# Dynamic weight builds of an attention + adapted FFN layer: every build group accumulated on DVE, DMA queue chosen by weight matrix instead of by parity

## The reference

```python
xn = layernorm(x)
out = x + attn(xn) + ffn(xn)

# attn: q, k, v = xn@wq, xn@wk, xn@wv; RMS norm over all 1024 of q and of k; 8 heads of 128;
#       each token sees itself and the 16 before it, ALiBi bias; softmax; (probs @ v) @ wo

# ffn, with weights of its own for every batch row:
h = relu(xn @ gate_w1.T + gate_b1)
g = (h @ gate_w2.T + gate_b2).mean(axis=1)          # (batch, 8)
mW1 = W1 + einsum('be,efh->bfh', g, TW1)            # 4096 x 1024, TW1 is (8, 4096, 1024)
mb1 = b1 + g @ Tb1
mW2 = W2 + einsum('be,ehf->bhf', g, TW2)            # 1024 x 4096, TW2 is (8, 1024, 4096)
mb2 = b2 + g @ Tb2
u = gelu(xn @ mW1.T + mb1)
ffn = u @ mW2.T + mb2
```

## Time and profile before

| | |
|---|---|
| time, median of 2 runs | 3646.16 us (3642.28 to 3650.03) |
| the profiled execution's own time | 3622.46 us |
| span of its slowest core, core 0 | 3620.6 us (all cores 3590.5 to 3620.6) |
| mean granted PE clock of the cores | 0.677 to 0.690 |
| busy on core 0: PE, DVE, ACT, POOL | 1204.2, 644.9, 658.7, 551.6 us |
| DMA | 475.37 MB, mean 131 GB/s |

### The profile page before, as it was taken

How to read it: one execution, slowest core, us unless ns; L and a number is a source line. 1 busy time by engine, 2 the same in 40 slices (tenths; PEclk the granted TensorE clock), 3 DMA queues, 4 the chain that set the end, 5 groups by cost and what they waited for, 6 DMA issues and landing times.

```text
span 3620.6 us, 18150 instructions; the slowest of 8 cores (3590.5 to 3620.6 us)
## 1 busy us (share of the span) xinstructions
PE 1204.2 (33%) x4955; PEld 491.3 (14%) x5044; DVE 644.9 (18%) x687; ACT 658.7 (18%) x1011; POOL 551.6 (15%) x267
## 2 busy tenths in 40 slices
PE   0333333523252326212622206000000065657565
PEld 0111111211020112100211002000000022222221
DVE  1010110222122212232132310222222200000000
ACT  1121211211222212122311122222222201011010
POOL 0000000011102210123011130344345300000000
PEclk9766666865675568555865558555555597979898
DMA  9222212043415340554034564887887746454544
GB/s 187 63 68 74 66 52 19 6 128 128 128 48 188 131 135 6 154 186 149 6 122 135 190 176 104 242 266 243 258 266 245 230 95 119 92 127 92 127 94 110
DMA packets 466039, 475.37 MB, mean 131 GB/s; under 512 B 362579, under 2 KB 362963, under 8 KB 465812
## 3 DMA queue, kind: packets, MB, share of 16 engines
q1 hardware_dynamic: 345060, 248.90, 24.9%
q10 hardware_dynamic: 116400, 214.81, 19.9%
q0 software_dynamic: 4480, 10.50, 1.9%
HBM read 357.91 MB, written 42.01 MB: 110 GB/s over the span
## 4 chain that ended last, share of the span: by engine, by line
DMA 27%; PE 26%; POOL 11%; DVE 10%; ACT 8%; SPq 7%; issue 6%; ACTq 5%; DVEq 0%; POOLq 0%
DMA O_s<-TW 15%; POOL accv_s L90 11%; SPq L95 7%; DMA O_s<-m2d 6%; PE pA L74 6%; ACTq L95 5%; PE pC L74 5%; PE pB L74 5%; PE pD L74 4%; PE pE L74 4%; PE pU L74 4%; DVE rz_s L90 3%; DVE accv_s L90 2%; DMA O_s<-xad 2%; DMA xnd<-xnb_s 2%
## 5 line engine op out<-in xcount | busy, mean ns | idle before, releaser
L90 POOL TENSOR_TENSOR accv_s<-bldt_s,accv_s 128x1024 f32<-128x1024 bf16 x224 | 477.9, 2133 | 2320.2 <-ACT bldt_s L85 2293.1
L85 ACT ACTIVATE bldt_s<-O_s,gbc_s 128x1024 bf16<-128x1024 f32 x256 | 293.0, 1147 | 1029.8 <-DMA O_s<-TW 573.5
L90 DVE SCALAR_TENSOR_TENSOR accv_s<-O_s,gbc_s,accv_s 128x1024 f32<-128x1024 f32 x224 | 287.7, 1284 | 754.8 <-DMA O_s<-TW 748.4
L74 PE MATMUL pA<-O_s 128*128 128x512 bf16 x624 | 194.4, 431 | 379.0 <-DMA O_s<-m1d 189.0
L74 PE MATMUL pA<-m2rowb_s,e0bf_s 128*128 128x512 bf16 x4 | 1.7, 428 | 636.8 <-DMA O_s<-m2d 633.2
L74 PE MATMUL pA<-O_s,selbf_s 128*32 128x512 bf16 x15 | 8.6, 571 | 554.0 <-ACT bldt_s L85 554.0
L74 PE MATMUL pB<-O_s 128*128 128x512 bf16 x631 | 179.6, 399 | 5.8 <-DMA O_s<-m2d 5.1
L90 DVE RECIPROCAL rz_s<-pE 1x512 f32<-1x512 f32 x32 | 104.9, 3314 | 375.5 <-PE pE L74 375.5
L74 PE MATMUL pC<-O_s,xt_s 128*128 128x512 bf16 x256 | 82.5, 480 | 242.3 <-DMA xt_s<-xnd 237.9
L85 ACT ACTIVATE O_s<-pA,mb_s 128x512 bf16<-128x512 f32 x64 | 44.0, 687 | 567.4 <-PE pA L74 564.2
L74 PEld LDWEIGHTS pA<-O_s 128*128 128x128 bf16 x640 | 65.9, 106 | 516.2 <-issue 473.2
(11 more groups left out here) (138 smaller groups left out, 1610.9 us busy)
## 6 DMA issues: line engine op xcount, KB each, us to landing
O_s<-TW ACTq DMA_DIRECT2D x256, 512.0 KB, 7.0
O_s<-TW SPq DMA_DIRECT2D x256, 512.0 KB, 5.6
O_s<-x SPq DMA_DIRECT2D x16, 1024.0 KB, 5.8
accv_s<-W SPq DMA_DIRECT2D x32, 512.0 KB, 5.5
accv_s<-W ACTq DMA_DIRECT2D x32, 512.0 KB, 5.0
xnd<-xnb_s ACTq DMA_DIRECT2D x32, 256.0 KB, 3.1
O_s<-x ACTq DMA_DIRECT2D x16, 512.0 KB, 3.6
xad<-O_s ACTq DMA_DIRECT2D x16, 512.0 KB, 2.8
```

Of the source, the lines that this page charges most:

```text
L74: i = self.eng.matmul(out, lhsT, rhs, start=start, stop=stop, skip_group_check=skip)
L85: i = self.eng.activation(out, in_, func, **kw) if self.on("scalar") else None
L90: i = getattr(self.eng, name)(*args, **kw) if self.on(who) else None
```

## The change

All groups now do their eight steps on DVE. The queue for a group's loads and store is SPq for the groups of `mW1` and ACTq for those of `mW2`. The `bldt` buffers go. Two accumulators, two output buffers and the ring of four slots stay. Apart from that, `gw1t` and `gb1r` get a semaphore of their own, `d_ldg2`, for which the gate's first matmul waits, and the wait for the rest of POOL's loads moves to `emit_g`.

```diff
@@ -30,7 +30,7 @@
 HS = HALO + SC
 
 SEM_NAMES = [
-    "d_ld", "d_ldg", "d_x0", "d_x1", "d_xw0", "d_xw1", "d_xt", "d_xtf",
+    "d_ld", "d_ldg", "d_ldg2", "d_x0", "d_x1", "d_xw0", "d_xw1", "d_xt", "d_xtf",
     "d_tw", "d_twp", "d_mwo", "d_mwop", "d_m10", "d_m11", "d_m20", "d_m21",
     "d_xr0", "d_xr1", "d_xa0", "d_xa1", "d_xf0", "d_xf1", "d_out0", "d_out1",
     "d_mb", "d_ts0", "d_ts1", "d_ts2", "d_ts3",
@@ -234,13 +233,13 @@
             cx.dma("gpsimd", s[n].rearrange("p (t d) -> p t d", d=D),
                    ap[n].rearrange("(t p) d -> p t d", p=128), "d_ldg")
         cx.dma("gpsimd", s["gw1t"].rearrange("p (t d) -> p t d", d=D),
-               ap["gw1tc"].rearrange("p (t d) -> p t d", d=D), "d_ldg")
+               ap["gw1tc"].rearrange("p (t d) -> p t d", d=D), "d_ldg2")
         cx.dma("gpsimd", s["gw2t"], ap["gw2tc"], "d_ldg")
         for nm in ("vhal", "gb1r", "rrows", "grow", "rz", "m2rowb", "expsh"):
             cx.vop("memset", s[nm], 0.0)
         bk["p0ms_v"] = cx.cnt["v"]
         cx.wait_at("gpsimd", "v", bk["p0ms_v"])
-        cx.dma("gpsimd", s["gb1r"][0:1, :], ap["gb1"], "d_ldg")
+        cx.dma("gpsimd", s["gb1r"][0:1, :], ap["gb1"], "d_ldg2")
         if P0SUB < 40:
             return
         cx.dma("sync", s["raw"][0:HALO, 1024:2048], ap["xhalo"], "d_mb")
@@ -330,7 +329,7 @@
                        ap["xnd"][gb * SC: gb * SC + HS, hc * 128:(hc + 1) * 128],
                        "d_xt", transpose=True)
             for st in range(4):
-                cx.wait("tensor", "d_xt", "d_ld", "d_ldg")
+                cx.wait("tensor", "d_xt", "d_ld", "d_ldg2")
                 cx.wait_at("tensor", "v", bk["p0ms_v"])
                 if gb or st:
                     cx.wait_at("tensor", "a", bk["relu_a"][-1])
@@ -375,6 +374,7 @@
         bk["hbred_v"] = cx.cnt["v"]
 
     def emit_g(cx):
+        cx.wait("tensor", "d_ldg")
         cx.wait("scalar", "t", "v")
         cx.act(s["hbarT"], s["hbacc"], AF.Identity, scale=1.0 / T)
         cx.wait("tensor", "a")
@@ -415,6 +415,7 @@
 
     def emit_build_group(cx, g):
         m1 = g < 32
+        q = "sync" if m1 else "scalar"
         if m1:
             ft = g
             wsrc = ap["W1"][ft * 128:(ft + 1) * 128, :]
@@ -428,17 +429,14 @@
         par = bk["bld_n"] % 2
         acc = s["accv"] if par == 0 else s["accv2"]
         outbuf = s["mwov"] if par == 0 else s["mwov2"]
-        q = "scalar" if par == 0 else "sync"
-        lsem = "v" if par == 0 else "p"
         wdsem = "d_tw" if par == 0 else "d_twp"
         osem = "d_mwo" if par == 0 else "d_mwop"
         slots = [s["twv"][:, r * D:(r + 1) * D] for r in range(4)]
-        asem, acnt = bk["acc_done"][par]
-        cx.wait_at(q, asem, acnt)
+        cx.wait_at(q, "v", bk["acc_done"][par])
         cx.dma(q, acc, wsrc, wdsem)
         wsem, wcnt = wdsem, cx.cnt[wdsem]
         i0 = bk["bld_idx"]
-        base = cx.cnt["v" if par == 0 else "a"]
+        v0 = cx.cnt["v"]
         for e in range(8):
             i = i0 + e
             r = i % 4
@@ -446,50 +444,31 @@
                 cx.wait_at(q, "v", bk["pa_end_v"])
                 cx.wait_at(q, "a", bk["pa_end_a"])
             elif e < 4:
-                ms, mc = bk["mac_cnt"][i - 4]
-                cx.wait_at(q, ms, mc)
+                cx.wait_at(q, "v", bk["mac_cnt"][i - 4])
             else:
-                cx.wait_at(q, "v" if par == 0 else "a", base + (e - 4) + 1)
+                cx.wait_at(q, "v", v0 + (e - 4) + 1)
             ssem = "d_ts%d" % r
             cx.dma(q, slots[r], twsrc[e], ssem)
             bk["slot_dma"][i] = (ssem, cx.cnt[ssem])
         for e in range(8):
             i = i0 + e
             ds, dc = bk["slot_dma"][i]
+            cx.wait_at("vector", ds, dc)
+            if e == 0:
+                cx.wait_at("vector", wsem, wcnt)
+                cx.wait_at("vector", "a", bk["gbc_a"])
+            cx.wait("vector", "v")
             out = acc if e < 7 else outbuf
-            if par == 0:
-                cx.wait_at("vector", ds, dc)
-                if e == 0:
-                    cx.wait_at("vector", wsem, wcnt)
-                    cx.wait_at("vector", "a", bk["gbc_a"])
-                cx.wait("vector", "v")
-                if e == 7 and bk["out_sem"][par] is not None:
-                    osm, ocn = bk["out_sem"][par]
-                    cx.wait_at("vector", osm, ocn)
-                cx.vop("scalar_tensor_tensor", out, slots[i % 4],
-                       s["gbc"][:, e:e + 1], acc, op0=ALU.mult, op1=ALU.add)
-                bk["mac_cnt"][i] = ("v", cx.cnt["v"])
-            else:
-                tmp = s["bldt0"] if e % 2 == 0 else s["bldt1"]
-                cx.wait_at("scalar", ds, dc)
-                pw = bk["pool_e"].get(e - 2 if e >= 2 else e + 6, 0)
-                if pw:
-                    cx.wait_at("scalar", "p", pw)
-                cx.act(tmp, slots[i % 4], AF.Identity, scale=s["gbc"][:, e:e + 1])
-                bk["mac_cnt"][i] = ("a", cx.cnt["a"])
-                cx.wait_at("gpsimd", "a", cx.cnt["a"])
-                if e == 0:
-                    cx.wait_at("gpsimd", wsem, wcnt)
-                cx.wait("gpsimd", "p")
-                if e == 7 and bk["out_sem"][par] is not None:
-                    osm, ocn = bk["out_sem"][par]
-                    cx.wait_at("gpsimd", osm, ocn)
-                cx.vop("tensor_tensor", out, tmp, acc, op=ALU.add, who="gpsimd")
-                bk["pool_e"][e] = cx.cnt["p"]
+            if e == 7 and bk["out_sem"][par] is not None:
+                osm, ocn = bk["out_sem"][par]
+                cx.wait_at("vector", osm, ocn)
+            cx.vop("scalar_tensor_tensor", out, slots[i % 4],
+                   s["gbc"][:, e:e + 1], acc, op0=ALU.mult, op1=ALU.add)
+            bk["mac_cnt"][i] = cx.cnt["v"]
         bk["bld_idx"] = i0 + 8
-        done = cx.cnt[lsem]
-        bk["acc_done"][par] = (lsem, done)
-        cx.wait_at(q, lsem, done)
+        done = cx.cnt["v"]
+        bk["acc_done"][par] = done
+        cx.wait_at(q, "v", done)
         cx.dma(q, dst, outbuf, osem)
         bk["out_sem"][par] = (osem, cx.cnt[osem])
         bk["bld_n"] += 1
@@ -990,8 +969,7 @@
                     "relu_a": [], "hbar_t": [], "xt_gate_t": [],
                     "group_out": {},
                     "bld_n": 0, "bld_idx": 0, "slot_dma": {}, "mac_cnt": {},
-                    "acc_done": {0: ("v", 0), 1: ("p", 0)},
-                    "out_sem": {0: None, 1: None}, "pool_e": {},
+                    "acc_done": {0: 0, 1: 0}, "out_sem": {0: None, 1: None},
                     "vq": 0, "hraw_a": [], "qraw_a": [], "kstt_v": [], "ppa": [],
                     "hbacc_v": [],
```

More of the change, by code:

```diff
@@ L168, in build_program @@
         ("accv2", (128, D), F32), ("mwov2", (128, D), BF16),
-        ("bldt0", (128, D), BF16), ("bldt1", (128, D), BF16),
     ]:
@@ L1003, in body @@
                 full_schedule(c)
-                if os.environ.get("K_CNT"):
-                    print("LANE", name, {k: v for k, v in c.cnt.items() if v})
             return body
```

## The result

The changed kernel takes 3476.42 us (median of 11 runs, 3460.39 to 3542.37) against 3641.6 us (median of 10). The ratio is 0.9555 with a 95% interval of 0.9518 to 0.9592: 4.45% less time. The forecast was 3490 on a before of 3646, a ratio of 0.957.

A forecast was written before the change was run, and what follows sets the result against it. No engine is full; each stage is bound by its serial chain. Terms -166 - 11 - 5 + 92 - 66 = -156 us take the median of 3646.16 to 3490, range 3440 to 3560, forecast chance 0.62.

The forecast's parts named there:

- Part 1: Attention tiles inside a chunk: builds take 34.1 us where 49.2 stood, gaining 15.1 x 11 = 166 us.
- The rival without head start: Attention tiles: first group not loaded ahead, each tile pays 2 x 20.9 us; total 3601 us, chance 0.08.
- Part 2: Three chunk boundaries: `xt` transposes run beside the builds, colliding for 8 us; 11 us gained in all.
- Part 3: Stretch between attention and the `mW2` builds: 189 us instead of 194, 5 us gained.
- Part 4: 32 `mW2` groups on ACTq: drained ring, 21.3 us each, plus 38 for transposes; 720 instead of 628, 92 lost.
- The term for the transposes: `mW2` builds: 24 early `m2t` transposes beside the loads cost 38 us, taken between 30 and 48.
- Three bursts of about 25 us: `mW2` stage: the early transposes run in three bursts of about 25 us each.
- The 36 us that I set beside my 38: `mW2` builds: by the skill's packet-by-packet rule, half-rate loads during 24 x 3 us of transposes cost about 36 us.
- Part 5: `ft` steps after the last `mW2` group: 24 issued early, leaving 35 us instead of 101.5; 66 gained.
- Edits at nothing: The `d_ldg` split at the start, the later chunks and POOL's silence beside DVE's steps: each given no effect.
- The slower rival: `mW2` groups at 28.4 us each through contention, total 3679 us; change loses from 27.4 a group; chance 0.03.
- The rival of `ft` steps that don't come early: After the `mW2` builds: early `ft` steps stay late, +54 instead of +26 us, total 3518; chance 0.10.

The follow-up runs named there:

- e5: Kernel before with only the queue of the `mW1` groups changed to SPq, odd groups still on ACT and POOL: 3630.12 us, ratio 1.0012.
- e2: The change with every `ft` transpose of the first FFN chunk waiting for all 32 groups: 3524.85 us, ratio 0.9629.
- e11: The change with each of the 24 early transposes issued twice, the second into an unused buffer: one run, builds 765.4 us.
- e6: The change with the first group's loads held until the first chunk's `xt` transposes landed: one run, 3519.48 us, first reciprocals at 708.8 instead of 716.8 us.
- e1: The change's DVE steps with each group's queue by parity again (even ACTq, odd SPq): 3453.8 us, ratio 0.9376.
- e4: Kernel before with the change made for the `mW1` groups alone (DVE steps and SPq): 3447.14 us, ratio 0.9439.
- e8: The change with stores issued after the next group's W and first four slices, and `ft` transposes waiting for all 32 groups: 3379.12 us, ratio 0.9325.
- e3: The change with each group's store issued after the next group's W and first four slices: 3410.0 us, ratio 0.9352.

## Why the prediction was right, step by step

The time, the sign and the main terms came out; the ratio was said within 0.002. Some of that is luck: parts 1 to 3 gained 36 us more than I had, part 4 and the start lost 25 more, and one term of part 4 was right for a wrong reason.

- **Part 1, attention tiles: right.** The reasons held one by one: PE no longer waits for `bldt` (e5 shows that this, and not ACT's queue, was the cause), the scores lie beside the builds, the first group runs on slices loaded ahead, the second on a drained ring. Both groups were sized 0.7 to 1.1 us too long: the 0.7 that I added to the second for a late first slice was not needed. 180 us instead of 166. The rival without head start is out (12.3 us).
- **Part 2, boundaries: mechanism right, size low.** The collision with the `xt` transposes was taken at 8 us from the earlier trace rows, and the groups were 5.4 longer (17.2 + 20.3 against 12.3 + 19.8). 26 us instead of 11.
- **Part 3: right in sign,** 12 instead of 5.
- **Part 4, the groups of `mW2`: the drained ring right, the collisions too small.** 21.3 a group was said, e2 gives 21.0. That it came so close is luck. I took off 2.5 us for 0.79 MB that the other queue moved beside the group of the earlier trace rows, its W and its store. In that window SP's queue moved 1.86 MB (the line is below this list), since the next group's slices go out from 2468.68 on; at 309 GB/s that is 6.0 us, and the same sum would have given 17.8. So a row with traffic beside it did not carry the term; e2's drained group with nothing beside it does. The term for the transposes was 38 and is 59 by e2, about 52 without the first eight groups. The core's own transposes cost 38 by the count under e11, as I had; the term that was mis-sized is what I put at nothing, the groups that have no transposes of their own, and what slows those stays open. "Three bursts of about 25 us" failed too: they last 50 to 70 us on core 5, since transposes are stretched by the loads as the loads are by them. The 36 us that I set beside my 38 were worked out with 3 us for a transpose in flight, which did not hold either.
- **Part 5, the `ft` steps: right,** 68 for 66.
- **Edits at nothing: one miss.** I took the gate's split for the only candidate at the start and did not count what SP now issues there. Group 0 moved from ACTq, where it had stood behind the first two tiles, to SPq, where its four slices go out at once, beside the `xt` transposes of the first chunk. The start was 8.6 us longer, 7 to 8 of it by this, and e6 takes it back.
- The slower rival, 27.4 us a group, was not approached: 22.9 with everything. The rival of `ft` steps that don't come early is out: PE's 200 matmuls stand in the window of the builds.

The queues of core 0 of the kernel before in the window of the earlier trace rows, 2451.2 to 2474.4 us (packets, MB, share of 16 engines; q10 is ACT's with its nine loads of 512 KB, q1 is SP's):

```profile
q10 hardware_dynamic: 1296, 4.72, 66.6%
q1 hardware_dynamic: 579, 1.86, 25.3%
```

What the sum did not show is how unequal the two halves of the change are. On `mW1` it gains about 210 us; on `mW2` e1 and e4 show that its queue costs more than it brings. DVE's steps with both queues and late `ft` steps would have taken 571 + 99 = 670 us there, against 732 + 31 = 763 in the change and 624 + 99 = 723 before. I had weighed the one queue against the kernel before only, not against the same steps on two queues.

The rule of the Trainium skill that I cited from "DMA: Bandwidth & Descriptors", "Issuing engines are not separate DMA queues", holds for the rate and not for the order: e1 and e2 load the same slices with the same engines of the chip, and differ by 102 us in the builds by which queue a store waits in. With the store issued behind the next loads, one queue comes near two: 599 us in e8 against 571 in e1.

## What to carry to other kernels

A store that waits for the last step of a piece of work, in the same in-order queue as the next piece's loads, empties the buffers once per piece: here 2 to 3 us of 21 in `mW2` (e8 and e1 against e2) and 4 of 20 in attention (e3). Issue it behind the next loads, or on another queue, before buying overlap elsewhere. An engine that mostly waits for DMAs may take over another engine's work at little cost, as DVE does here, and what is then gained is the other engine's place in the chain. When a group of loads moves to another queue, ask for the first one of them too: what had held it back, and what it now runs beside.

## What the runs showed that I had not expected

The price of a transposing DMA beside loads was not one number: 1.6 us for each of the core's own in the change, 2.8 with the store deferred (e3), where the loads leave fewer gaps, and the boundaries became 6 us longer each although the builds in them did not get more work. Doubling the transposes (e11) cost 33 us where removing them (e2) gave 59, but 14 of the 26 between them arise in the first eight groups, before the first transpose: a stretch that an edit cannot reach is a measure of noise that every trace carries with it, and it should be read first. In e5, taking two fifths off one group's time and adding over a quarter to the other's left the whole at a ratio of 1.0012, so a null result can hold two effects that are each worth some 6 to 8 us a tile.
